# Gathers of a sparse two-layer graph attention: which table row the empty edge slots read

## The reference, cut to what matters

```
h  = relu(layernorm(x))
s  = h @ W0 @ inp.T                               # M x N scores
x  = x + softmax(where(adj > 0, s, pad) / 0.07) @ inp
h  = relu(layernorm(x)) @ W1
e  = leaky_relu(h @ a_src + (h @ a_dst).T)        # M x N
w  = softmax over the neighbours of e, cut below 0.0001, times the number of neighbours
x  = x + elu(h + w @ h)
```

## Time and profile before

| | us |
|---|---|
| median of 3 runs | 753.84 (750.98 to 756.42) |
| profiled execution | 758.33 |
| its span | 756.7 |
| DVE busy in the span | 521.8 (69%) |
| ACT busy | 410.8 (54%) |
| PE busy | 413.3 (55%) |
| POOL busy | 366.3 (48%) |

### The profile page before, as it was taken

How to read it: one execution, slowest core, us unless ns; L and a number is a source line. 1 busy time by engine, 2 the same in 40 slices (tenths; PEclk the granted TensorE clock), 3 DMA queues, 4 the chain that set the end, 5 groups by cost and what they waited for, 6 DMA issues and landing times.

```text
span 756.7 us, 9557 instructions
## 1 busy us (share of the span) xinstructions
PE 413.3 (55%) x2947; PEld 276.4 (37%) x2947; DVE 521.8 (69%) x1921; ACT 410.8 (54%) x424; POOL 366.3 (48%) x424
## 2 busy tenths in 40 slices
PE   3433646566667676767675846647360520416654
PEld 1010213244444343435352524426260520415654
DVE  0019596889898988979893958949822532639994
ACT  4458677777878788888856758662300110012122
POOL 5000140607070606151573765748887887878700
PEclk9577787788988899879795879976565555566786
DMA  8999799999999999999999999932121232223422
GB/s 326 430 412 419 262 305 352 341 352 319 351 353 334 363 336 348 357 349 332 371 321 290 319 306 321 336 110 57 38 59 46 57 76 52 44 58 88 124 83 74
DMA packets 37478, 186.78 MB, mean 247 GB/s; under 512 B 7856, under 2 KB 8112, under 8 KB 18864
## 3 DMA queue, kind: packets, MB, share of 16 engines
q1 hardware_dynamic: 28208, 167.02, 58.8%
q0 software_dynamic: 9216, 19.11, 12.0%
HBM read 179.73 MB, written 6.37 MB: 246 GB/s over the span
## 4 chain that ended last, share of the span: by engine, by line
DVE 30%; POOL 21%; DMA 18%; issue 12%; ACT 9%; PE 8%; SPq 0%; POOLq 0%; DVEq 0%; ACTq 0%
DMA arena<-in_adj 18%; POOL arena L819 12%; ACT arena L873 7%; PE K L1424 4%; POOL mean_w L814 3%; DVE keys L1029 2%; POOL E L819 2%; POOL X L790 2%; DVE s_e L1136 1%; POOL arena L790 1%; DVE mi_w L1175 1%; DVE RTp L1194 1%; PE G L1635 1%; ACT R_all L902 1%; DVE G L1135 1%
## 5 line engine op out<-in xcount | busy, mean ns | idle before, releaser
L873 ACT ACTIVATE arena<-arena,half_c 128x2048 bf16<-128x2048 int32 x144 | 284.5, 1999 | 88.0 <-DMA arena<-in_adj 77.2
L790 POOL DMA_INDIRECT X<-in_L_gnn_input,idx_all x132 | 131.8, 998 | 299.7 <-DVE idx_near L1108 233.9
L1424 PE MATMUL K<-arena,bits 128*128 128x512 bf16 x576 | 174.0, 443 | 22.6 <-ACT arena L873 22.4
L819 POOL DMA_INDIRECT arena<-table,idx_near x96 | 99.5, 1036 | 28.5 <-issue 22.2
L1424 PEld LDWEIGHTS K<-arena,bits 128*128 128x128 bf16 x576 | 60.2, 110 | 97.3 <-ACT arena L873 31.0
L1029 DVE MAX8 keys<-K 128x8 int32<-128x128 f32 x192 | 42.4, 281 | 56.7 <-PE K L1424 56.7
L1422 PE MATMUL K<-key_add,key_one 128*128 128x512 bf16 x48 | 22.4, 466 | 57.8 <-DVE keys L1029 32.1
L819 POOL DMA_INDIRECT E<-table,idx_near x48 | 47.0, 979 | 14.4 <-issue 12.2
L1436 PE MATMUL G<-g,R_all 128*128 128x128 bf16 x324 | 25.3, 228 | 39.3 <-DVE s_e L1136 26.0
L1099 DVE COPY led<-SA 128x396 f32<-128x396 f32 x12 | 6.8, 570 | 56.0 <-PE SA L1482 56.0
L814 POOL MEMSET mean_w<- 128x512 f32 x72 | 38.5, 535 | 2.1
(11 more groups left out here) (245 smaller groups left out, 1031.6 us busy)
## 6 DMA issues: line engine op xcount, KB each, us to landing
arena<-in_adj SPq DMA_DIRECT2D x144, 1024.0 KB, 9.3
table<-hs SPq DMA_DIRECT2D x12, 262.0 KB, 9.1
hs<-table SPq DMA_DIRECT2D x12, 262.0 KB, 2.8
E<-in_L_gnn_input SPq DMA_DIRECT2D x1, 3072.0 KB, 23.9
out_x<-x_all SPq DMA_DIRECT2D x12, 256.0 KB, 2.1
x_all<-in_x SPq DMA_DIRECT2D x1, 2560.0 KB, 17.4
X<-in_L_gnn_input,idx_all POOLq DMA_INDIRECT x132, 6.0
arena<-table,idx_near POOLq DMA_INDIRECT x96, 2.7
```

The costliest lines, as they stand in the source:

```text
L790: pool.indirect_dma_start(out=x_of(b)[:, e, :], out_offset=None, in_=inp, in_offset=bass.IndirectOffsetOnAxis(ap=idx_all[:, at:at + 1], ax ...
L819: pool.indirect_dma_start(out=E[g][:, t, :], out_offset=None, in_=tables[g], in_offset=bass.IndirectOffsetOnAxis(ap=idx_near[:, t, g:g + 1 ...
L873: nc.scalar.activation(sign[:, load % RING, :], ring[:, load % RING, :], ACT.Sign, bias=half_c[:], scale=1.0).then_inc(signed, 1)
L1424: last = mm(bank_[:], bits[:, third * TB + j, :], sign[:, load % RING, j * FOLD:(j + 1) * FOLD], start=False, stop=(third == G - 1 and j = ...
```

## The change

Two tiles of 128 x 12 are added. `spare_row` is filled once by POOL: 1 + b + 2048 g + 15 p for partition p, tile b of the batch and third g. In `columns_of_edges` two DVE steps are added: `no_edge` is `spare_row` where `idx_f` is 0, and 0 elsewhere, and is added to `idx_f`. The maximum in the step that writes `idx_all` goes. So a slot with no edge reads row 2048 g + b + 15 p of `inp` and row b + 15 p of table g; at most 3 + 15 x 127 = 1908, inside the third. Within one gather these rows all differ; they are the same in every batch.

```diff
+        spare_row = sb("spare_row", [P, B, G])
+        no_edge = sb("no_edge", [P, BG])
...
+                pool.iota(spare_row[:], pattern=[[1, B], [THIRD, G]], base=1, channel_multiplier=15,
+                          allow_small_or_imprecise_dtypes=True)
...
                     link(nc.vector.reduce_sum(idx_f[:, 0:n_e], pick[:, 0:n_e].rearrange("p e c s -> p e (c s)"), AX))
-                    ts(idx_all[:, edges(b)], idx_f[:, 0:n_e], 1.0, -1.0, ALU.max, ALU.add)
+                    link(stt(no_edge[:, 0:n_e], idx_f[:, 0:n_e], 0.0,
+                             spare_row[:, 0:size].rearrange("p b g -> p (b g)"), ALU.is_equal, ALU.mult))
+                    link(tt(idx_f[:, 0:n_e], idx_f[:, 0:n_e], no_edge[:, 0:n_e], ALU.add))
+                    ts(idx_all[:, edges(b)], idx_f[:, 0:n_e], -1.0, None, ALU.add)
```

## The result

The changed kernel takes 731.95 us (730.28 to 736.16, 4 runs) where the kernel before takes 755.13 us (750.98 to 757.09, 4 runs): ratio 0.975, 95% interval 0.971 to 0.979. The profiled execution took 731.36 us, its span 729.5.

The account below looks back on a forecast made before the run. It took DVE's loop, then loads of adj in the last three turns, to bound stage one, with stage two following; DVE's steps of 2.0 + 0.4 + 0.4 = +2.8 us on 753.84 gave 756.6 us, range 741 to 763.

Parts of the forecast that it names:

- Two limits in turn: Stage one: DVE's loop bounds the 39.0 us turns, loads of adj the last three turns of 45.4 to 47.9 us.
- DVE's steps: Index work of stage one: two added chained steps cost 0.40 us a turn, +2.8 us in all, bounds +2.0 to +4.4.
- POOL's iota: Constants ahead of the first turn: one more iota costs nothing, at most its own 0.3 us.
- its issue: POOL's queue: same number of gathers and rows, nothing moved past a queue, so no cost.
- landing in stage two: Gathers of stage two: sooner landing saves 0 to 0.4 us, taken as 0.
- Where 43 of 128 slots read: Gathers in the three load-bound turns: between 21.7 us less and 11.7 us more, taken as 0.
- Rival B: Load-bound turns: reads of row 0 queue in HBM and slow adj loads too; full size 736 us, chance 0.26.
- B's sign: Load-bound turns: under Rival B, loads beside gathers would cost under 43 engine-us per MB.
- B2: Load-bound turns: row 0 slows only the gathers that read it; at most 9.9 us less, 746.7 us, chance 0.15.
- C: Last three turns: fresh rows cost more than a repeated one; full size 11.7 us more, 768.3 us, chance 0.10.

Follow-up runs that it names:

- f1: Changed kernel with spare_row filled with 1, so both DVE steps run but all empty slots read row 0: 754.22 us, 1.005 of the kernel before.
- a2: The changed kernel unedited, run a third time, in another series against the kernel before: 731.82 us, ratio 0.976.
- f4: Changed kernel with all empty slots of one gather reading one row, another for each of a batch's 12 gathers: 732.15 us, 0.976 of the kernel before.
- e7: Changed kernel with spare_row stepping by 1 per partition instead of 15, so empty slots read neighbouring rows: 731.75 us, 0.973 of the kernel before.
- a1: The changed kernel unedited, run again in another series against the kernel before: 733.44 us, ratio 0.976.
- f2: Changed kernel with only gathers of inp reading rows of their own, record gathers reading row 0: 739.19 us, 0.988 of the kernel before.
- g4: Changed kernel's rows with one chained DVE step fewer, on a chip where the kernel before took 758.82 us: ratio 0.997.

## Why the prediction was wrong

1. **Two limits in turn, DVE's loop and then the loads.** Right in the main. The three load-bound turns fell to 39.9, 38.5 and 37.5 us once loads came faster, about the length of DVE's loop (38.6 us a turn in the same trace). The landing of `adj` left most of the chain, but the DMA engines stayed 98% busy, so both limits are close to one another there.
2. **DVE's steps, +2.8 us.** Right in size: 0.41 us a turn in the trace, f1 costs 4 us, between 1 and 7, and its five middle turns take 39.4 us, as forecast.
3. **POOL's iota, its issue, and landing in stage two at nothing.** Right within 2 us: the rest of the span from the hand-over on is 1.8 us shorter.
4. **Where 43 of 128 slots read, taken as 0.** This is the step that failed: the sum has 0 for it, and the rows alone are worth 22.4 us between f1 and a2, 22.8 us in the load-bound turns of the profiled pair. It compared a gather alone (4.4 engine-us) with a gather beside loads (4.8) and concluded that row 0 could not be a pile-up. The runs show both halves of that to be weak. Over all load-bound turns a gather cost 5.4, not 4.8; the stretch picked was one of the cheaper ones (the turn around it, 411 to 456 us, has 5.3, the one before it 5.6). And a gather alone is no floor for one under load: with the rows spread it costs 3.3 beside the loads. In the changed kernel, alone, from 535 to 565 us:

```profile
q0 software_dynamic: 640, 1.32, 17.3%
...
arena<-in_L_gnn_input,idx_all POOLq DMA_INDIRECT x12, 2.5
```

That is 4.2 engine-us for each of 20 gathers, against 4.4. So in this pair spreading saves 6% when nothing else runs and 39% under load. With nothing else running f1, with row 0, has 4.7 (553 to 583 us), so row 0 costs 0.2 to 0.5 there against about 2 beside loads. f4, with one row inside a gather, has 5.0 alone (540 to 570 us), which is 0.8 above the changed kernel, though beside loads it is only 0.3 above; why is open. What the 4.2 consists of no run tells; it could neither prove nor exclude a pile-up under load.

The end that the prediction kept for this term, 21.7 us less, is about what came: 22.8 us in those turns of the profiled pair, which has a long execution of the kernel before. Rival B had this end and 0.26; its full size is 17.7 us less than the kernel before, and the medians lie 23.2 us apart. In the profiled pair the missing part is spread out: the five middle turns, held to cost 0.4 us more each, cost 0.4 us less; the last three are 2.3 us shorter than B has them; and the span behind the hand-over is 1.8 us shorter. The first of these did not come again everywhere: the middle turns take 38.6 us in the changed kernel and e7, 38.9 and 39.2 in a1 and a2, but 39.5 in f2 and f4, whose gathers of `inp` read spread rows or changing rows too. Why they are short in the first is open.

B's sign that loads would cost under 43 engine-us per MB came (41.4), but f1, which reads row 0, has 42.6, so it is a weak sign: the part of the loads in the gain is 1 to 3 engine-us per MB. B2, which left the loads alone, had at most 9.9 us less and is too small; gathers' own time makes up 3.2 of 7.6 us a turn. C is out: fresh rows cost less, not more.

The prediction set the Trainium skill, DMA: Bandwidth & Descriptors, Latency and other measured facts, against its own choice: where lock-step streams fall on rows a large power of two apart, the rate halves. The runs bear out the direction that the prediction drew from it (0.975), not the page's case, which none of them has: here it is one repeated row, and rows side by side are as good as rows far apart. Whether channels are the reason no run tells.

## What to carry to other kernels

Slots of an indirect gather that are padding should not all read one row: with a third of the slots at one row and a load stream beside them, a gather cost 5.4 engine-us in place of 3.3 and the kernel 2.4% of its time, on the chips where loads bound it. For that time it was enough that gathers behind one another read different rows, by a constant that changes from gather to gather; a row for each slot costs the same two DVE steps here and a little less engine time (3.3 against 3.6). Do not read the price of contention from a quiet stretch or from one short busy one, and where a series shows no gain at all, look whether the kernel before is slower there too.

## What the runs showed of the hardware

Reads of one row of 512 B, 43 in a gather and a gather each 1.25 us, slow the gathers (5.1 to 5.7 engine-us against 3.2 to 3.3) and also the loads of other memory beside them (42.6 to 44.3 engine-us per MB against 41.4 to 41.6). The row may be any: 5.7 with row 3000 of `inp` and row 1000 of the table. With another row in each gather the same 43 reads cost 3.6. With nothing beside them the price is smaller (4.4 and 4.7 against 4.2 in single stretches of 30 us). On two of the four chips engines stop for up to 6.3 us at a time at waits named "remote" (g4), and there the 2.4% does not show (0.997); why is open.
